# Attention of a four-block model rebuilt: keys by pairs of heads in row groups, one maximum per half of heads, plain fp32 projections, expert tiles of 256 rows

## The reference

```python
x = x + tanh(g_xattn[0]) * L0_xattn(layernorm(x), ctx)      # 16 heads of 16, scale 1/4, biases on q, k, v, o
x = x + tanh(g_ffn[0])   * L0_ffn(layernorm(x))             # real(ifft(fft(x) @ w)) + bias: one 256x256 matrix
x = x + tanh(g_xattn[1]) * L1_xattn(layernorm(x), ctx)      # 16 heads of 16, relative position bias, no scale
x = x + tanh(g_ffn[1])   * L1_ffn(layernorm(x))             # top 2 of 8 experts, hidden 512, squared relu
```

## Time and profile before

| what | us |
|---|---|
| median of 3 runs | 2338.26 |
| lowest and highest | 2338.23, 2343.16 |
| profiled execution, its own time | 2336.51 |
| its span in the trace | 2334.3 |
| PE busy | 1909.4 (82%) |
| DVE, ACT, POOL busy | 1248.1, 733.1, 931.8 |

### The profile page before, as it was taken

How to read it: one execution, slowest core, us unless ns; L and a number is a source line. 1 busy time by engine, 2 the same in 40 slices (tenths; PEclk the granted TensorE clock), 3 DMA queues, 4 the chain that set the end, 5 groups by cost and what they waited for, 6 DMA issues and landing times.

```text
span 2334.3 us, 43845 instructions
## 1 busy us (share of the span) xinstructions
PE 1909.4 (82%) x13810; PEld 1693.3 (73%) x13811; DVE 1248.1 (53%) x3412; ACT 733.1 (31%) x1461; POOL 931.8 (40%) x1286
## 2 busy tenths in 40 slices
PE   2698988988889888898898988987089888888884
PEld 1687877878778788787787877877077776777773
DVE  2356566666665666666656666554544333333331
ACT  2122223232232322323223223222344444444432
POOL 1334445354353543535445354352223333333333
PEclk7799999999999999999999999989599999999997
DMA  4101101011010110101101001010533333333332
GB/s 115 21 13 34 32 12 44 12 33 33 17 38 12 32 35 18 35 14 30 35 18 35 22 23 40 13 32 19 176 66 61 59 59 58 57 56 59 59 50 30
DMA packets 186837, 93.65 MB, mean 40 GB/s; under 512 B 119832, under 2 KB 180248, under 8 KB 186808
## 3 DMA queue, kind: packets, MB, share of 16 engines
q1 hardware_dynamic: 160648, 57.40, 10.3%
q0 software_dynamic: 26160, 35.87, 8.9%
HBM read 43.77 MB, written 44.39 MB: 38 GB/s over the span
## 4 chain that ended last, share of the span: by engine, by line
PE 43%; DMA 18%; issue 13%; POOL 9%; ACT 8%; DVE 7%; SPq 1%; POOLq 0%; DVEq 0%; ACTq 0%
PE scores L1083 23%; DMA out<-y,ids 16%; PE bank L1083 15%; POOL sorted_rows L680 5%; PE bank L1147 2%; ACT routed L790 2%; ACT t_hi L755 2%; POOL rstd L627 2%; DVE t_lo L900 1%; DVE biased L965 1%; ACT q_hi L760 1%; PE bank L1291 1%; POOL kb_hi L645 1%; ACT pr L773 1%; DMA raw<-w_down_t 1%
## 5 line engine op out<-in xcount | busy, mean ns | idle before, releaser
L708 POOL DMA_INDIRECT out<-y,ids x136 | 211.6, 1556 | 458.2 <-ACT y L814 270.6
L627 POOL TENSOR_TENSOR rstd<-var,half_power 128x2 f32<-128x2 f32 x128 | 90.1, 704 | 567.1 <-DVE var L887 566.4
L1083 PE MATMUL scores<-vb,pr 128*128 128x136 f32 x2048 | 285.3, 282 | 19.3 <-ACT pr_rest L776 19.3
L1083 PEld LDWEIGHTS scores<-vb,pr 128*128 128x128 f32 x2048 | 260.4, 192 | 24.9 <-issue 21.3
L1067 DVE SCALAR_TENSOR_TENSOR h<-scores,relu 128x512 f32<-128x512 f32 x136 | 94.0, 691 | 272.7 <-ACT relu L808 272.7
L938 DVE TENSOR_REDUCE mx<-scores 128x8 f32<-128x512 f32 x256 | 169.5, 683 | 117.0 <-PE scores L1083 117.0
L755 ACT ACTIVATE t_hi<-bank 128x512 fp32r<-128x512 f32 x192 | 114.8, 598 | 357.0 <-PE bank L1147 357.0
L1083 PE MATMUL scores<-q_hi,kb_hi 128*128 128x256 f32 (+1 forms) x640 | 198.1, 310 | 34.5 <-ACT neg_mx L765 34.5
L900 DVE TENSOR_TENSOR t_lo<-bank,t_hi 128x512 fp32r<-128x512 f32 x192 | 132.0, 687 | 130.2 <-ACT t_hi L755 126.4
L680 POOL DMA_INDIRECT sorted_rows<-routed,place x128 | 126.5, 988 | 151.6 <-ACT routed L790 120.5
L1083 PE MATMUL scores<-up_hi,xt_hi 128*128 x272 | 120.4, 443 | 79.4 <-DVE xt_lo L1061 78.9
(11 more groups left out here) (219 smaller groups left out, 5460.0 us busy)
## 6 DMA issues: line engine op xcount, KB each, us to landing
xe<-sorted_rows SPq DMA_DIRECT2D x136, 128.5 KB, 2.0
x<-x_rows SPq DMA_DIRECT2D x32, 256.0 KB, 3.0
out<-x_end SPq DMA_DIRECT2D x32, 256.0 KB, 3.1
vb<-v_main SPq DMA_DIRECT2D x128, 32.0 KB
vr<-v_rest SPq DMA_DIRECT2D x256, 3.2 KB
raw<-w_up_t SPq DMA_DIRECT2D x8, 512.0 KB, 4.6
raw<-w_down_t SPq DMA_DIRECT2D x8, 512.0 KB, 4.6
out<-y,ids POOLq DMA_INDIRECT x136, 3.8
```

The costliest lines, as they stand in the source:

```text
L627: pool.tensor_tensor(rstd[u][:], var[u][:], half_power[:], ALU.pow).then_inc(sem(f"rstd_ready{u}"), 1)
L708: pool.indirect_dma_start(out=acc, out_offset=bass.IndirectOffsetOnAxis(ap=ids[j][:], axis=0), in_=y[j][:], in_offset=None, compute_op=ALU ...
L1083: last = pe.matmul(dst, w, m, start=n == 0, stop=n == len(pairs) - 1)
```

## The change

- Projections, keys and values are plain fp32 matmuls, without a split of weights or of inputs; `turn_low`, `split_ctx` and all `w_lo`, `c_lo`, `t_lo` go.
- Scores: an instruction contracts over 32 partitions (a row group j, the two heads of a pair), four neighbours have four row groups and write four PSUM banks. `by_query` (per g, half of the heads) makes all 77 keys of both heads for both query tiles in the four banks, DVE reduces them in one instruction of 128 x 1232, and the second g has to wait for that reduction, since it writes the same banks. `by_key` makes the first 128 of the 154 keys of a pair, `by_key_rest` the last 26 of four pairs (104 rows).
- The order: six slots instead of ten; turn and output stand in one slot between the two `by_query`; the queries of the next half are the last thing in a half.
- The value tiles are 77 rows per unit and written straight into `vb`; the bias tables are made after the second half of the first pair, not before part 1; `vb` is cleared early.
- Part 2: tiles of 256 rows, worked off as two blocks of 128; NT = 72 tiles, 144 blocks; POOL waits for `added` at every second block; 18 instead of 9 scatters of zero rows.

```diff
 def half(...):
-            do["queries"](*a)
-            fill(1)
-            do["by_token"](*a, 0)
-            ...
+            do["by_query"](u, t, l, 0)
+            fill(1)
+            do["by_query"](u, t, l, 1)
+            fill(2)
+            do["turn_max"](u, t, l)
+            do["by_key"](u, t, l)
+            do["exp"](u, t, l, 0)
+            do["exp"](u, t, l, 1)
+            fill(3)
+            do["by_key_rest"](u, t, l)
+            do["exp"](u, t, l, 2)
+            fill(4)
+            do["sums"](u, t, l, 0)
+            fill(5)
+            do["sums"](u, t, l, 1)
+            fill(6)
 def ffn_steps(u, t):
+            return {1: [("turn", "a0", u, t), ("output", 0, u, t)], 2: [("norm", 1, u, t)],
+                    3: [("turn", "t1", u, t)], 4: [("ffn", u, t), ("norm", 2, u, t)],
+                    5: [("turn", "t2", u, t)], 6: [("queries", u, t, 1), ("queries_low", u, t, 1)]}
 PE, rows_by:
-                    last = product(bankB[:, c * D:(c + 1) * D],
-                                   [(m[:, k, part], n[:, w, k]) for k in range(NK) for m, n in passes(t_hi[u], t_lo[u], w_hi, w_lo)])
+                    last = product(bankB[:, c * D:(c + 1) * D], [(turned_x[u][:, k, part], w[:, n, k]) for k in range(NK)])
 PE, by_query (one g):
+                clear("scores", t)
+                if l == 1:
+                    for j in range(NJ):
+                        pe.matmul(sc[:, j, 0:NC * PK], ident_b[:], bias_t[:, g, :, j * PK:(j + 1) * PK], start=True, stop=False)
+                for c in range(NC):
+                    for j in range(NJ):
+                        rows = slice(2 * DH * j, 2 * DH * (j + 1))
+                        last = pe.matmul(sc[:, j, c * PK:(c + 1) * PK], q_hi[u][rows, g, c * P:(c + 1) * P], kb_hi[rows, l, g, u],
+                                         start=l == 0 and c == 0, stop=c == NC - 1)
 PE, by_key:
+                if l == 1:
+                    for j in range(NJ):
+                        for b_ in (bias_hi, bias_lo):
+                            pe.matmul(sc[:, j], ident_r[:], b_[:, j].rearrange("p g t -> p (g t)"), start=b_ is bias_hi, stop=False)
+                for g in range(G):
+                    for n in range(3):
+                        for j in range(NJ):
+                            rows = slice(2 * DH * j, 2 * DH * (j + 1))
+                            k_, q_ = passes(kb_hi[rows, l, g, u, 0:P], kb_lo[rows, l, g, u, 0:P], q_hi[u][rows, g], q_lo[u][rows, g])[n]
+                            pe.matmul(sc[:, j, g * T:(g + 1) * T], k_, q_, start=l == 0 and g == 0 and n == 0, stop=False)
+                pe.wait_ge(sem("neg_mx_ready"), so_far("max", t))
+                for g in range(G):
+                    for c in range(NC):
+                        for j in range(NJ):
+                            ...
+                            last = pe.matmul(sc[:, j, g * T + c * P:g * T + (c + 1) * P], expand[rows, c, 0:P], neg_mx[u][rows, g], ...)
 POOL, part 2:
-                    pool.wait_ge(sem("added"), k * (DEEP * 16) + j * 16)
+                    if j % NB == 0:
+                        pool.wait_ge(sem("added"), k * (DEEP * 16) + j * 16)
```

More of the change, by code:

```diff
@@ L46 @@
 TURNS = ("t0", "a0", "t1", "t2", "a1", "t3")
+EACH = {"t0": 6, "t1": 6, "k0": 1, "k1": 1, "q0": 2, "q1": 2, "rows": 8, "v0": 4, "v1": 4, "gate": 2, "ranks": 2,
+        "max": 4, "rest": 4, "scores": 12}
 def buckets(distance):
@@ L287, in wait, with since, so_far @@
                 engine.wait_ge(sem(name), value)
-        def half(do, a, early, slots):
-            def fill(slot):
-                for stage, *args in slots.get(slot, ()):
+        def since(t, per, value):
+            return value if isinstance(t[0], int) else t[0] * per + value
+        made = {}
+        held = {}
+        def so_far(what, t, each=1, less=0):
+            return since(t, each * EACH[what], each * made[what] - less)
+        COUNTED = {"keys": lambda l, t: f"k{l}", "turn": lambda name, u, t: f"t{u}", "queries": lambda u, t, l: f"q{u}", "values": lambda u, t: "rows",
+                   "output": lambda l, u, t: "rows", "ffn": lambda u, t: "rows", "sums": lambda u, t, l, c: f"v{u}", "gate": lambda u, t: "gate",
+                   "places": lambda u, t: "ranks", "turn_max": lambda u, t, l: "max", "by_key_rest": lambda u, t, l: "rest",
+                   "by_query": lambda u, t, l, g: "scores", "by_key": lambda u, t, l: "scores"}
@@ L295, in fill, with half @@
+        STAGES = ("queries", "queries_low", "by_query", "turn_max", "by_key", "by_key_rest", "exp", "sums", "turn", "output", "norm", "ffn", "gate",
+                  "choose", "columns", "weights", "places", "weigh", "send", "stats0", "spread", "keys", "values", "values_out", "loads", "load_x",
+                  "store_x", "tables", "bias")
+        def half(do, u, t, l, slots):
+            def fill(n):
+                for stage, *args in slots.get(n, ()):
                     do[stage](*args)
-            do["queries"](*a)
+            do["by_query"](u, t, l, 0)
@@ new lines, in count, with counted, first_half @@
+            def count(stage):
+                run_stage = do.get(stage, lambda *args: None)
+                what = COUNTED.get(stage)
+                def counted(*args):
+                    if what is not None:
+                        made[what(*args)] += 1
+                    run_stage(*args)
+                return counted
+            made.update(dict.fromkeys(EACH, 0))
+            held.clear()
+            do = {stage: count(stage) for stage in STAGES}
+            def first_half(t, *more):
+                half(do, 0, t, 0, steps(*more, {4: [("values", 1, t), ("values_out", 1, t)]}, start_steps(1, t), {3: [("keys", 1, t)], 4: [("spread", 1, 0, t)], 6: [("spread", 1, 1, t)]}))
@@ L1140, in turn @@
+            def turn(name, u, t):
                 if name[0] == "a":
@@ L1223, in sums @@
[L1223 to L1234 removed]
+                hold("B", f"q_lo_ready{u}", f"q{u}")
@@ L1259, in _ @@
+                "turn_max": turn_max, "by_key": by_key, "by_key_rest": by_key_rest, "sums": sums, "gate": gate, "places": places,
             }, pe.Fori)
```

837 lines of the change are left out of this document (371 added, 466 removed).

## The result

The changed kernel takes 2480.1 us (2474.0 to 2486.2) beside 2339.0 us of the kernel before: 1.060 times as long, interval 1.057 to 1.063. The forecast was 2287 and faster. Its profiled execution has a span of 2479.7 us, against 2334.3.

The account below looks back on a forecast made before the run. PE was taken to bound part 1 and the scatters part 2. Span 2334.3 - 31 (setup) + 64 (part 1) - 93.7 (part 2) + 11.4 (zero rows) = 2285, with 2.2 around it 2287 us; range 2160 to 2480, 8 in 10.

Parts of the forecast that it names:

- The clock: Part 1's loop: PE's holes lower the granted clock in most halves, soon made good; 3.4 us a pair, bounds 0 and 17.
- Rival 2: Part 1's loop: the clock stays down, costing the full 17 us; period 114 to 117, 2500 to 2550 us; chance 0.11.
- PE's work: Part 1, per pair: PE's work falls from 77.6 to 69 us.
- The row groups: Part 1: 224 row-group instructions a pair at 0.045 us, 10 us; bounds 6.3 and 25.3.
- the ledger of the kernel before: Part 1 before, per pair: 77.6 us of PE work from counts and prices; the rest of 96.2, 18.6, is waiting and latency.
- The waits: Part 1, per pair: PE waits about 28 us against 18.6 before, 13 of it ahead of `turn_max`.
- Period: Part 1's loop: 100.2 us a pair, +4, over 16 pairs +64 us; wrong if under 90 or above 106.
- the two first suspects: Part 1: what to doubt first if the period left its band: the price of a row group and the clock.
- Part 2: Two scatters under way, PE sets the pace at 3.70 us a block; 545.4 us instead of 639.1, gain 93.7.
- Zero rows: Ahead of part 2: 9 more scatters of zero rows at 1.265 us each, +11.4 us.
- Setup: Before the loop: keys begin near 35 us instead of 67.15; sum -31 us.
- Chances: Whole kernel: faster 0.59, same 0.03, slower 0.38; the forecast itself has 0.50.

Follow-up runs that it names:

- e7_places: The changed kernel with `weigh` and `places` moved behind the output projection in slot 1: 2388.3 us, 1.021 of the kernel before.
- e8_places_fill: e7_places with 22, 32, 18 and 18 unread matmuls in the holes ahead of `turn_max`: 2338.3 us, 1.000 of the kernel before.
- e11_hole_long: The kernel before with an unread DVE reduction of 3584 elements ahead of handing on the first maxima in each half: 2601.8 us, 1.112.
- e5_part2: The kernel before with only part 2 of the change (256-row tiles, scatters in couples, 18 zero-row scatters): 2262.7 us, 0.968.
- e2_order: The changed kernel with DVE alone doing slot 1 behind the second maximum: 2480.3 us, 1.061 of the kernel before.
- e9_rest_first: e7_places with the score matmuls of `by_key_rest` ahead of `turn_max` and the turned maxima in another bank: 2452.0 us, 1.048 of the kernel before.
- e12_hole_short: The kernel before with an unread DVE reduction of 1280 elements ahead of handing on the first maxima in each half: 2392.4 us, 1.022.
- e10_keys_too: e9_rest_first with the keys of the next pair also moved ahead of `turn_max`, to slot 2: 2413.3 us, 1.032 of the kernel before.
- e6_whole: The changed kernel with its score matmuls contracting over all 128 partitions instead of row groups of 32 (another output): 2655.7 us, 1.136 of the kernel before.
- e4_each: The changed kernel with every scatter of part 2 waiting for the one before it again: 2616.1 us, 1.118 of the kernel before.

## Why the prediction was wrong

**The clock, the step that failed.** I took 3.4 us a pair, between bounds of 0 and 17, as "a fall in most halves that is soon made good". Measured 12.7. The falls came in all four halves, and they were not soon made good: 30.7 of 112.6 us passed at 1.2 GHz. The row I had of it said just that: a fall after 3.71 us idle, and a slow rise. I named a hole of 3.0 to 3.6 us, called it near that, and then chose a value close to the bound of nothing. What the runs showed in its place: a clock term of 12.7 us, which went to 8.7 when two waits shrank (e7_places) and to 3.3 when the holes were filled (e8_places_fill), and which e11_hole_long brought about in the loop of the kernel before. Rival 2, the clock stays down, had period 114 to 117 and a chance of 0.11. Its mechanism is the one that came true, its price of 17 us was 4.3 too high, and the period of 112.6 came within 1.4 us of it because PE's work was 4.2 us more than forecast. The error of 9.3 us a pair is 149 us over 16.

**PE's work.** Forecast 69, measured 73.2 at full clock. The row groups were right, even a little dear: 224 took 8.7 us in e8_places_fill, 0.039 each, where I took 0.045. What was short are the other terms: I priced each matmul by the dense middle of a run. Rows of the changed kernel at full clock, eight instructions of a projection and four turns, from start to next start:

```profile
753.51 0.65 PE L1074 MATMUL bank<-ident,xn 128*128 128x128 f32 x4
754.86 1.99 PE L1013 MATMUL bank<-w,turned_x 128*128 128x256 f32 x8 [0.69 <-ACT turned_x L713]
756.69 0.17 PE L1209 MATMUL bank<-hot_sum,before_b 128*128 128x16 bf16 x1
```

1.83 / 8 = 0.229 an instruction of a projection, not 0.213, and (754.86 - 0.69 - 753.51) / 4 = 0.165 a turn, not 0.1. Over a pair: projections +1.5, turns +1.8, biases +1.0, `by_key_rest` +0.6, sums +0.3, row groups -1.4. The same error sat in the ledger of the kernel before (77.6 forecast, 85.4 measured), where it was harmless, because the waits there were what was left over (18.6 forecast, 10.7 measured) and the sum closed by construction. For the kernel after both were my own, and nothing closed them. Cost: 4.2 us a pair, 67 over 16.

**The waits.** 28 forecast, 26.7 measured, and the largest as laid out: 13 us ahead of `turn_max`, 13.2 measured. Not foreseen: the 4.0 us at `places` and `weigh`. They took the place of what I had too much elsewhere, so that the sum is right in part by luck. And the comparison was not right: idle time rose by 16.0 against the kernel before, where I had +9.4.

**Period.** 100.2 + 9.3 + 4.2 - 1.3 = 112.4, of 112.6. Over 16 pairs the three differences are 149 + 67 - 21 = 195 us, and the span is 195 above the 2285 of the sum. That they meet so exactly is chance, since the 6 us of part 2 (below) are not among the three. The period left the band of 90 to 106 that I had given, and of the two first suspects the clock was one; the price of a row group was innocent.

**Part 2.** As forecast in kind and nearly in size: scatters in couples, 143 x 3.711 us from the first relu to the last (3.70 forecast). First block to the end 551.5, where I had 545.4; the 6 us are the last scatters (16.0 us from the last relu to the end, not 11.5) and the 0.011 a block. e5_part2 shows part 2 alone: the 2262 worked out from the trace beforehand, 2262.7 measured. The scatters in pairs of starts, in the changed kernel:

```profile
1953.37 1.56 POOL L680 DMA_INDIRECT out<-y,ids  x1 [3.10 <-DMA out<-y,ids]
1955.99 1.56 POOL L680 DMA_INDIRECT out<-y,ids  x1 [1.06 <-ACT y L774]
1960.67 1.56 POOL L680 DMA_INDIRECT out<-y,ids  x1 [3.13 <-DMA out<-y,ids]
```

The first of a couple waits 3.1 us for a landing, the second 1.0 for its own `y`: 7.3 us a couple, PE's time for two blocks. Zero rows: 18 scatters, 1.27 us from start to start, as taken.

**Setup.** The keys began at 32.2 (35 forecast). But of the 35 us by which they began earlier only 18.7 were left at the first load of x inside the loop (I had 31), most likely since the two halves of the prologue have the loop's holes and its low clock: from 78.7 to 112.8 us the clock fell three times and was low for 20.5 us, where the kernel before had one fall of 13.7 (82.3 to 96.0). The loss was not taken apart further.

**Chances.** 0.59 for faster rested on a clock term that I set near its lower bound without a row for it. With 3.4 replaced by the middle of its own bounds, 8.5, the same sum gives 2369 us, 1.3% slower than before.

## What to carry to other kernels

A long enough wait of PE had two prices here: its length, and the work behind it at half speed. A change that takes work from PE and gives it holes can lose both ways; here 12.2 us less work a pair brought 16.0 more idle time and 12.7 of clock. Before removing work from the bounding engine, ask what it covered, and where a forecast hole is of like length as one behind which a row shows a fall, count the fall. Closing one hole with work taken from another place only moves it (e2_order, e9_rest_first); look at the sum of idle time, not at one wait. And where two changes come together, price and run them apart: the second part of this one alone is 3.2% faster than the kernel before. Which of part 1's own changes (row groups, plain fp32, the order in six slots) pays and which costs, no run here separates.

## What the runs showed of the hardware

- The changed loop has six falls of the clock a pair. Four lie at the holes ahead of `turn_max`, of 2.7 to 4.6 us. One lies at the wait of 1.36 us for `hot_sum`, which follows one of 0.61 by 0.45 us (723.8, rows at e7_places); the wait of 2.61 us behind it was already at the low clock. One lies behind three short waits, as in these rows of e7_places, where waits of 1.55, 0.85 and 0.77 us stand within 10 us:

```profile
737.56 0.66 PE L1074 MATMUL bank<-ident,xn 128*128 128x128 f32 x4 [1.55 <-DVE xn L845]
743.12 0.70 PE L1116 MATMUL scores<-bias_t,ident_b 128*128 128x308 bf16 x4 [0.85 <-ACT q_hi L718]
745.55 1.79 PE L1013 MATMUL bank<-w,turned_x 128*128 128x256 f32 x4 [0.77 <-ACT turned_x L713]
```

```profile
736.00:745.90 9.90, 6.74 (x51) 5.51 (x51) 4.37 (x9) 2.03 (x4) 4.62 (x5) 1.00 0.15 53
745.90:749.30 3.40, 3.40 (x10) 2.40 (x9) 0.12 (x1) 0.00 (x0) 0.00 (x0) 0.50 0.00 0
```

  PE was busy for 6.74 of 9.90 us ahead of that fall. It is not a matter of the longest wait alone.
- A wait of some 2 us was near the edge. e12_hole_short waits for `hot_sum` in every pair, for up to 2.0 us, and in these six pairs none of the waits brought the clock down (total us, times, longest):

```profile
PE bank L1252 <- DVE hot_sum L986: 17.0, 12, 2.0
```

  Over its whole loop the clock fell at five of these waits (1.86 to 2.12 us), each time for 3.4 us, and held at the others, 1.26 to 2.04 us long. In e5_part2, whose part 1 is that of the kernel before, it fell at two, of 1.74 and 2.08 us, and held at another of 2.08. The kernel before, with no wait over 1.46 us in its loop, had no fall there.
- A low stretch lasted 3.4 to 6.8 us in the changed kernel, up to 10.2 in e9_rest_first and 13.7 in e10_keys_too. PE was busy for 25.4 of the 30.7 us a pair that the changed kernel passed in them.
- At 1.2 GHz PE's work takes 1.8 to 2.0 times as long. From start to next start, medians of the changed kernel: the instructions of a projection 0.427 and 0.216 us, those of `sums` 0.227 and 0.116, turns 0.213 and 0.109, four row groups 0.21 to 0.22 and 0.12 (rows at e6_whole). So the cost of a fall is close to half of the time that PE works in it.
- Four fp32r matmuls of four row groups, of 256 columns and with a weight load of 128 columns each, start within 0.11 to 0.12 us (707.53, 707.65), the price of one whole matmul: the four overlap wholly. The Trainium skill, "TensorEngine Tiling (Array Packing)", Key Properties, says that different tiles can run weight loads and matmuls in parallel; the trace agrees. The same place names a drain at a change of mode. Of that the rows show 0.2 us at most: the first four of `by_key` start 0.33 us behind the whole matmul ahead of them (706.98 and 707.31; 0.24 between the two ahead), and 0.22 us before the next four (707.53), where the others take 0.12. That this is the drain no run here shows.
- One scatter of 128 rows into DRAM keeps the next one waiting some 3 us after its 1.56 us of issue. Two under way cost 7.3 us a couple, which is PE's pace, where two single ones cost 9.2 (e4_each). Among the last scatters, which wait for no block, a couple took 6.5 us (2464.80 to 2471.26), near the 6.4 that the prediction gave for POOL alone:

```profile
2464.80 1.56 POOL L680 DMA_INDIRECT out<-y,ids  x1 [3.49 <-DMA out<-y,ids]
2466.82 1.56 POOL L680 DMA_INDIRECT out<-y,ids  x1 [0.47 <-issue]
2471.26 1.56 POOL L680 DMA_INDIRECT out<-y,ids  x1 [2.87 <-DMA out<-y,ids]
```
